# AdaLN, path attention and a routed FFN on one core: the chosen-expert operand made through DRAM and a VectorE product instead of TensorE transposes

## The reference, cut to what matters

```python
h   = relu(x @ w_down[b]) @ w_up[b] + x                 # conditioned adapter
phi = features(sigmoid(h @ Wp + bp))                    # 8 heads, depth 5 -> 32 features
ctx = softmax(causal(phi_q . phi_k)) @ (h @ Wv)
x   = x + ctx @ Wo
# second half
y      = x @ (U[b] @ V) + bias[b]                       # U is 256 x 30, so y has rank 30
z      = x @ U[b] + ub[b]                               # 30 numbers a token
chosen = argmax(y @ gate_w.T)                           # one of 8 experts
x      = x + y + y @ expert_w[chosen].T                 # = x + (z times one-hot(chosen)) @ G, with G 8*30 x 256
```

## Time and profile before

| | before |
|---|---|
| median of three runs | 143.74 us |
| the profiled execution | 143.52 us |
| its span, first to last instruction | 141.8 us |
| TensorE busy | 134.9 us (95%) |
| VectorE busy | 97.3 us (69%) |
| ScalarE, GpSimd busy | 60.8 us, 37.7 us |
| granted TensorE clock | 1.000 |

### The profile page before, as it was taken

How to read it: one execution, slowest core, us unless ns; L and a number is a source line. 1 busy time by engine, 2 the same in 40 slices (tenths; PEclk the granted TensorE clock), 3 DMA queues, 4 the chain that set the end, 5 groups by cost and what they waited for, 6 DMA issues and landing times.

```text
span 141.8 us, 4892 instructions
## 1 busy us (share of the span) xinstructions
PE 134.9 (95%) x2174; PEld 85.4 (60%) x2174; DVE 97.3 (69%) x180; ACT 60.8 (43%) x76; POOL 37.7 (27%) x62
## 2 busy tenths in 40 slices
PE   7998989999999979999999999999999999999992
PEld 6864665555555846565556765656567674656550
DVE  1354576694988953999475949797677957988621
ACT  3011644755864516563553366265426365410010
POOL 5000029103054531520333625201266630200000
PEclk9999999999999999999999999999999999999999
DMA  4899989910022000000111000001101010111122
GB/s 133 289 472 441 414 341 346 350 42 0 7 35 35 5 5 0 0 5 0 44 37 41 1 5 0 32 10 40 41 5 37 5 37 5 39 42 37 42 74 74
DMA packets 7285, 12.63 MB, mean 89 GB/s; under 512 B 1488, under 2 KB 5712, under 8 KB 7136
## 3 DMA queue, kind: packets, MB, share of 16 engines
q1 hardware_dynamic: 7264, 12.32, 24.5%
HBM read 10.10 MB, written 2.22 MB: 87 GB/s over the span
## 4 chain that ended last, share of the span: by engine, by line
PE 85%; DVE 8%; ACT 3%; issue 2%; POOL 0%; ACTq 0%; POOLq 0%
PE work L662 36%; PE s_ps L662 25%; PE c_ps L662 19%; DVE rden L492 2%; PE work L881 2%; ACT prob L431 2%; DVE tiles L603 2%; DVE h_t L538 1%; PE work L820 1%; DVE tiles L605 1%; PE work L873 1%; PE s_ps L881 1%; DVE ctx_t L493 1%; PE work L780 1%; ACT phi_t L454 0%
## 5 line engine op out<-in xcount | busy, mean ns | idle before, releaser
L431 ACT ACTIVATE prob<-s_ps 128x1536 f32<-128x1536 f32 (+1 forms) x24 | 38.3, 1595 | 30.8 <-PE s_ps L662 30.8
L400 POOL TENSOR_SCALAR_AFFINE_SELECT prob<-prob 128x1024 f32<-128x1024 f32 x16 | 18.6, 1160 | 75.4 <-ACT prob L431 75.4
L492 DVE RECIPROCAL rden<-c_ps 128x256 f32<-128x256 f32 x16 | 28.1, 1755 | 6.9 <-PE c_ps L662 6.9
L662 PE MATMUL s_ps<-phi_t 32*128 32x256 f32 (+1 forms) x384 | 24.2, 365 | 0.6 <-ACT prob L431 0.3
L662 PEld LDWEIGHTS s_ps<-phi_t 32*128 32x128 f32 x384 | 17.4, 184 | 9.8 <-issue 8.0
L662 PE MATMUL c_ps<-prob,v_sb 128*32 128x256 f32 (+1 forms) x384 | 22.1, 347 | 0.0
L662 PEld LDWEIGHTS c_ps<-prob,v_sb 128*32 128x32 f32 x384 | 11.0, 109 | 9.3 <-issue 3.7
L662 PE MATMUL work<-vl_sb,h_t 128*32 128x296 f32 x208 | 15.1, 415 | 0.4 <-DVE h_t L538 0.4
L662 PE MATMUL work<-ctx_t,mix_sb 128*32 128x256 f32 x176 | 11.6, 381 | 0.5 <-ACT zo_t L474 0.5
L662 PE MATMUL work<-zo_t,gexp 128*32 128x256 f32 x176 | 11.5, 379 | 0.0
L603 DVE TENSOR_TENSOR tiles<-tiles,prob 128x1024 f32<-128x1024 f32 x8 | 9.7, 1218 | 1.5 <-POOL prob L400 1.5
(11 more groups left out here) (119 smaller groups left out, 167.8 us busy)
## 6 DMA issues: line engine op xcount, KB each, us to landing
wdec<-in_W_dec SPq DMA_DIRECT2D x1, 3855.0 KB, 18.6
x_t<-in_x_tr SPq DMA_DIRECT2D x4, 512.0 KB, 7.9
ex_t<-in_expert_tr SPq DMA_DIRECT2D x1, 2048.0 KB, 23.2
out_x<-x_t SPq DMA_DIRECT2D x16, 128.0 KB, 1.7
mix_sb<-in_mix SPq DMA_DIRECT2D x1, 949.0 KB, 8.9
lift_sb<-in_lift SPq DMA_DIRECT2D x1, 384.0 KB, 3.3
vl_sb<-in_vl SPq DMA_DIRECT2D x1, 316.0 KB, 6.3
first_sb<-in_first SPq DMA_DIRECT2D x1, 144.0 KB, 2.2
```

Of the source, the lines that this page charges most:

```text
L400: nc.gpsimd.affine_select(out=tri, in_=tri, compare_op=ALU.is_ge, fill=0.0, base=0, pattern=[[0, HG], [0, 2], [1, P]], channel_multiplier= ...
L431: nc.scalar.activation(prob[:, p % 2, :, 0:width(p)], s_ps[:, :, 0:width(p)], ACT.Exp).then_inc(exped, 1)
L492: link(nc.vector.reciprocal(rden[:], c_ps[m % 2][:, CW:2 * CW]))
L662: return nc.tensor.matmul(o, w, r, start=start, stop=stop, skip_group_check=True)
```

## The change

The choice and z are stored to DRAM and read back spread over the partitions, and VectorE multiplies them (`zm`), for sequences 0 to 2. `zs` loses the transpose of z and its copy; a new step `pT` transposes `pick` alone. `zo` on GpSimd and `zoT` on TensorE and ScalarE go for these sequences. Beside that: the copy of `WoU` moves from VectorE to ScalarE and `zT` waits for it only half-way; the prologue has another order and two zero matmuls less; `VL` waits for one half of `h_t`; the last output block is split in two.

```diff
-PROLOGUE = [("gdn", (0,)), ("gup", 0), ("gdn", (1, 2, 3)), ("down", 0), ("ugT", 0), ("up", 0, 0), ("up", 0, 1), ("gup", 1),
+PROLOGUE = [("gdn", (0,)), ("gdn", (1, 2, 3)), ("gup", 0), ("ugT", 0), ("down", 0), ("gup", 1), ("up", 0, 0), ("up", 0, 1),
...
+        gaps[3] += [("zm", prv, 0)] if prv >= 0 else []
         gaps[3] += [("feat", n1, ALL_T)]
...
-        gaps[1] += [("zs", prv, ALL_T), ("zo", prv, 0), ("zo", prv, 1), ("VL", n1, 1)]
+        gaps[1] += [("zs", prv, ALL_T), ("VL", n1, 1)]
...
-    if prv >= 0:
-        gaps[3] += [("zoT", prv, 0), ("zoT", prv, 1)]
+    if prv >= 0 and n1 == B:
+        gaps[3] += [("zm", prv, 0)]
...
+    if prv >= 0:
+        gaps[1].insert(0, ("pT", prv))
+        gaps[3].append(("zm", prv, 1))
...
-          ("out", B - 1, 1), ("zoT", B - 1, 1), ("out", B - 1, 2), ("out", B - 1, 3)]
+          ("out", B - 1, 1), ("zoT", B - 1, 1), ("out", B - 1, 2), ("out", B - 1, 3), ("out", B - 1, 4)]
...
+def place(b, i):
+
+    if b < B - 1 or i < 3:
+        return i % DC, CW * (i // DC), CW
+    return 1, CW + P * (i - 3), P
...
+                elif s[0] == "zT" and s[1] < B - 1:
...
+                    done(sp, s)
+                    sp.dma_start(z_dram.rearrange("t k q -> (t k) q"), z_t[:]).then_inc(z_stored, 16)
+                elif s[0] == "pT":
...
+                    sp.dma_start(pick_dram.rearrange("e g t q -> (e g t) q"), pick_t[:]).then_inc(pick_stored, 16)
+                    sp.wait_ge(z_stored, 16 * (b + 1))
+                    for e in range(HG):
+                        sp.dma_start(z_rep[KP * e:KP * (e + 1), :].rearrange("k (t q) -> k t q", t=TT),
+                                     z_dram.rearrange("t k q -> k t q")).then_inc(z_spread, 16)
+                    sp.wait_ge(pick_stored, 16 * (b + 1))
+                    for e in range(HG):
+                        sp.dma_start(pick_rep[KP * e:KP * (e + 1)],
+                                     pick_dram[e].rearrange("g t q -> g (t q)").unsqueeze(0).broadcast_to([KP, 2, T])
+                                     ).then_inc(pick_spread, 16)
...
+                elif s[0] == "WoU":
+                    full(act, s)
+                    nc.scalar.copy(wo_u[:].rearrange("p c n -> p (c n)"), bank(s)[:, 0:DC * P]).then_inc(empty(s), 1)
...
+                    nc.scalar.copy(pick_t[:], bank(s)[0:TT * E, 0:P]).then_inc(empty(s), 1)
...
+                elif kind == "zm":
...
+                    dve.wait_ge(z_spread, 16 * HG * (b + 1))
+                    dve.wait_ge(pick_spread, 16 * HG * (b + 1))
+                    if b >= 1:
+                        full(dve, ("out", b - 1, 2 * hf + 1))
+                    nc.vector.tensor_tensor(zo_t[:, :, half], z_rep[:, half].unsqueeze(1).broadcast_to([P, 2, CW]),
+                                            pick_rep[:, :, half], ALU.mult).then_inc(zo_made, 1)
...
-                    for _ in range(3):
+                    for _ in range(1):
...
-                        done(pe, ("up", b, 0))
-                        done(pe, ("up", b, 1))
+                    if t % 2 == 0:
+                        done(pe, ("up", b, t // 2))
...
-                        done(pe, ("ubT",))
-                        done(pe, ("WoU",))
+                        pe.wait_ge(u_ready, 1)
                     for c in range(2 * DC):
+                        if c == DC and b == 0:
+                            done(pe, ("WoU",))
...
+                elif kind == "pT":
+                    pe.wait_ge(picked, s[1] + 1)
+                    ins = nc.tensor.transpose(o[0:TT * E, 0:P], pick[:], ident[:])
```

More of the change, by code:

```diff
@@ L319, in build @@
         zo_ready = sem("zo_ready")
+        z_stored = sem("z_stored")
+        pick_stored = sem("pick_stored")
+        z_spread = sem("z_spread")
+        pick_spread = sem("pick_spread")
+        zo_made = sem("zo_made")
         chain_v = sem("chain_v")
@@ L409, in _ @@
                                                 ).then_inc(mixed, 1)
[L410 to L416, removed]
-                    ins.then_inc(zo_ready, 1)
         @block.scalar
@@ L576, in _ @@
                     ins.then_inc(u_ready, 1)
-                elif kind == "WoU":
-                    full(dve, s)
-                    nc.vector.tensor_copy(wo_u[:].rearrange("p c n -> p (c n)"), bank(s)[:, 0:DC * P]
-                                          ).then_inc(empty(s), 1)
                 elif kind == "G":
@@ L638, in _ @@
                     full(dve, s)
-                    c, half = i % DC, slice(CW * (i // DC), CW * (i // DC + 1))
-                    nc.vector.tensor_tensor(x_t[:, b, c, half], bank(s)[:, 0:CW], x_t[:, b, c, half], ALU.add
+                    c, lo, n = place(b, i)
+                    half = slice(lo, lo + n)
+                    nc.vector.tensor_tensor(x_t[:, b, c, half], bank(s)[:, 0:n], x_t[:, b, c, half], ALU.add
                                             ).then_inc(empty(s), 1)
@@ L690, in product @@
             def product(b, i, c):
-                row, half = slice(P * (i % DC), P * (i % DC + 1)), slice(CW * (i // DC), CW * (i // DC + 1))
+                d, lo, n = place(b, i)
+                row, half = slice(P * d, P * (d + 1)), slice(lo, lo + n)
                 w = wo[:, c, row] if c < DC else gexp[:, c - DC, row]
                 r = ctx_t[:, b % 2, c, half] if c < DC else zo_t[:, c - DC, half]
-                return tiled(bank(("out", b, i))[:, 0:CW], w, r, start=(c == 0), stop=(c == 2 * DC - 1))
+                return tiled(bank(("out", b, i))[:, 0:n], w, r, start=(c == 0), stop=(c == 2 * DC - 1))
             def denominators(p):
@@ L889, in _ @@
                     for c in range(DC if ("wo", b, i) in ORDER else 0, 2 * DC):
-                        if c == DC:
-                            done(pe, ("zoT", b, i // DC))
+                        if c == DC and b == B - 1:
+                            done(pe, ("zoT", b, place(b, i)[1] // CW))
+                        elif c == DC:
+                            pe.wait_ge(zo_made, 2 * b + i // DC + 1)
                         ins = product(b, i, c)
```

55 lines of the change are left out of this document (38 added, 17 removed).

## The result

The changed kernel takes 145.35 us, the median of five runs (144.99 to 145.69), against 143.25 us (142.90 to 143.91, five runs) for the kernel before: a ratio of 1.0137, 95% interval 1.0099 to 1.0176. The forecast was 143.5, with a range of 141.8 to 145.2; the time lies above it, beside the rival "late data" (145.8). Executions can fall into a slower state, mostly with a mean granted clock of 0.988 in place of 1.0; medians in this document are over all runs, ratios over the fast ones.

What follows compares the result with a forecast made beforehand. TensorE was taken as the bound, with VectorE second and as good as first from pair 9 to 11. Terms -1.1 - 0.4 + 0 + 0.2 + 0.2 + 1.2 - 0.3 = -0.2 gave 143.5 us, range 141.8 to 145.2.

Steps and rivals of the forecast that it cites:

- late data: Rival: DMA chain exceeds its 6.3 us cover, first zm holds VectorE's work behind it; +2.3, 145.8 us; chance 0.17.
- The DMA path: Store and loads of choice and z ahead of first zm: 5.2 us chain within 6.3 us of cover, costing nothing.
- Transposes out: Sequences 0 and 1: zo transposes (1.0 us TensorE) removed, 0.6 kept, but each stage ends +0.2 later through the collision.
- no collision: Rival: zm and select overlap or select falls ahead; 0.7 kept in each of two stages; -2.3, 141.4 us; chance 0.22.
- The collision: At pairs 11 and 17: GpSimd's select and VectorE's second zm or addition run one after the other; stage +0.2 (0 to +0.4).
- an idle of over 1 us ahead of pairs 11 and 17: Sign that the forecast is right: TensorE idle this long ahead of the denominators of these pairs.
- `pT` replaces the transpose of z "one for one": Sequences 0 and 1, TensorE: the new transpose of pick takes the place of z's transpose, one for one.
- The last stage: Sequence 3's stage: pick wait +0.4, zo_t wait -0.2, second zm +0.65, bank +0.35; +1.2 (+0.5 to +1.6).
- The second product: Last stage: the second zm puts 0.65 into VectorE's full queue ahead of zo of sequence 3.
- `WoU`: Ahead of zT of sequence 0: copy on ScalarE, no TensorE wait for it; -1.1 (-0.9 to -1.2).
- The prologue: Opening: first VL waits for one addition to h_t, 0.65 less, against 0.25 more for gup 1; net -0.4 (0 to -0.65).
- The tail: End: half-width last addition, 0.41 to about 0.3, and last store with half the bytes; -0.3 (0 to -0.5).

Runs made afterwards that it cites:

- no_wait: Changed kernel with all DMAs still issued, but VectorE multiplies constant tiles and waits for no DMA (other output); 146.66 us, ratio 1.0224.
- zm1_late: early_z with the product for the second half of the tokens moved behind the closing additions of pairs 11, 17 and 23; 145.03 us, ratio 1.0124.
- hybrid: early_z with the DMA path for sequences 0 and 1 alone, second product behind closing additions, end banks two turns later; 141.81 us, ratio 0.9872 to before.
- no_select: early_z without the affine selects of pairs 11, 17 and 23 (pairs left unmasked, other output); median 143.86 us of two runs, no ratio.
- pt_late: moved_all with sequence 2's second product back ahead of pair 23's opening addition and its pT behind the following output; 144.16 us, ratio 1.0045.
- bank3: early_z with the turn of the six banks at the end starting three later; 144.56 us, ratio 1.0061 to the kernel before.
- moved_all: early_z with both the second product moved as in zm1_late and the banks as in bank3; 144.38 us, ratio 1.0078.
- early_z: Changed kernel with z's four loads issued right behind z's store, ahead of the store of the choice; 144.78 us, ratio 1.0081.

## Why the prediction was wrong, step by step

- **The DMA path, "cost it at nothing": this step failed.** The cover was 6.4 us (56.12 to 62.56), as forecast; the chain was put at 5.2 and took 7.7, 7.8 and 7.3. Two terms were mis-sized: the issues, taken at 0.33 and a gap from a plain store, were 0.47 each, and in two stages one of them 1.68 or 1.31; and the landing, taken at 1.7, was 2.7 in the median and up to 4.1. One wait was wrong: the loads of the choice were to start when its store had landed (1.7), but in all three stages they started behind the loads of z in SyncE's queue (58.41 - 56.15 = 2.3 in the first). The rival "late data" is what happened, but that its 7.8 us fits the 7.7 measured is luck: it had 3.3 for both landings, and measured were 1.4 and 2.7, with slow issues between them. Its price in sequence 1's stage was 0.93 (no_wait) where the rival had 1.5, in the next 0.14, in the last 0.09 (7.92 against 7.83). That is 1.2 us of the 2.4 by which the sum was off.
- **Transposes out.** That they buy nothing was right: TensorE waits for the sum of pair 9 (0.56), and the stretch from `zT` to there is 11.70 against 11.72. Of the 0.6 to 0.7 a stage that the prediction had as kept without a collision, zm1_late, hybrid and no_select leave 0.07 to 0.10: the rival "no collision" was too large as well.
- **The collision** was right in kind and too small: with data in time (no_wait) the stages end 0.40 and 0.39 later than before, against +0.2. The forecast had the select wait for VectorE. Where the select starts first, it is VectorE's product that is stretched; where the product starts first, the select and then the addition. The stages lost about the same in both orders (15 to 17: 9.90 less 0.14 of late data in the kernel after, 9.76 in no_wait). The marker "an idle of over 1 us ahead of pairs 11 and 17" did not come; TensorE had spent its lead earlier, at `zo_t` (0.51) and at a bank (0.74).
- **The rules for the collision.** The section VectorE Performance Modes of "Advanced Engine Details and Errata" of the Trainium skill names only the two-port modes; read alone, as the prediction read it, it has nothing collide, and no_select shows that something does. (The same page, under GPSIMD Details, counts VectorE instructions with two SBUF inputs among the conflicts.) "SBUF — State Buffer" of the Trainium skill (SBUF: two separate sides) has the one that starts second wait for the whole of the first; the 1.01, 1.49 and 2.12 us agree with it to about 0.15 us.
- **`pT` replaces the transpose of z "one for one"** was wrong: the stretch of the last stage shows +0.64, of which pt_late gives back 0.49 when the wait for `pick` is gone. What remains is 0.15, and its cause was not tried; the transpose of the choice itself takes 0.20 from start to start (111.71 to 111.91). In the stages before it is hidden.
- **The last stage,** +1.2 forecast, measured 0.64 + 0.76 = 1.4. The wait for `pick` is worth 0.49 (0.4 forecast) and the bank 0.25 to 0.28 (0.35). The second product, 0.65 forecast, shows no price of its own: bank3 and moved_all differ in its place and have 7.58 both. Beside bank and late data 0.42 are left, and they are the choice's small steps meeting the select of pair 23 three steps earlier than before. So the total of this term is near, with a part of it wrong.
- **`WoU`,** -1.1: -1.07. **The prologue,** -0.4: the edit is worth -0.17, and x landed 0.28 later in this execution. The gain of 0.65 by the shorter wait was largely given back, since `gup` 1 and its VectorE work stand ahead of `h_t` now: `h_t` starts 3.22 behind `down` (11.05), where it was 2.80 (10.35), against the 0.25 estimated. **The tail,** -0.3: -0.1.

The errors by terms, in the traces: prologue +0.5, stage 1 +1.1, stage 2 +0.3, last stage +0.2, tail +0.2: together 2.4, which is the distance from -0.2 to +2.2.

## What to carry to other kernels

A round trip through DRAM is not one store and one load: count each issue in the queue that carries it, take the slowest landing of the trace for loads that decide a start, and ask for cover that holds then. Here 7.3 to 7.8 us were needed for two hops with eight loads.

TensorE work that is removed ahead of a wait pays only what the wait leaves; look first at what releases the next instruction. And when a step is moved, list who reads its result as well as who stands behind it on its engine.

## What the runs showed of the hardware

- An affine select on GpSimd (1.10 us) and a float32 VectorE operation with both inputs in SBUF overlap by no more than some 0.15 us, whichever starts first: 0.69 became 1.01 and 1.49, and 1.22 became 2.12, and without the select both went back. An addition with one input in PSUM (68.50, in the kernel after) kept its 0.41 us beside a select.
- Issues of one kind in one queue are not all alike: of the twelve loads of the choice the median one took 0.43 us and one 1.68; of those of z one took 1.31. What holds a single issue was not found.
- The same load of 128 KB landed after 2.4 to 4.1 us in the kernel after; a store of 64 KB after 1.5 to 1.8 us there and once, in early_z, after 3.0 us. The cause was not tried.
